# Output projection of an attention layer: from four fp32 products on token chunks to three two-part products with stationary weights

## The reference, cut to what matters

```
q, k, v = (split_heads(layernorm(x) @ W) for W in (Wq, Wk, Wv))
attn = softmax(q @ k.T + bias)
ctx = (attn @ v)                 # per head 512 x 64, 16 heads: 512 x 1024
x = x + ctx @ Wo                 # Wo: 1024 x 128
```

## Time and profile before

| | |
|---|---|
| runs timed | 1105.16 us median of 3 (1104.22 to 1105.43) |
| the profiled execution's own time | 1105.33 us |
| its span, first to last instruction | 1103.4 us |
| attention steps 0 to 63 | from 16.4 to about 780 us of the span |
| expert blocks | from there to the end |
| mean granted TensorE clock | 0.985 |

### The profile page before, as it was taken

How to read it: one execution, slowest core, us unless ns; L and a number is a source line. 1 busy time by engine, 2 the same in 40 slices (tenths; PEclk the granted TensorE clock), 3 DMA queues, 4 the chain that set the end, 5 groups by cost and what they waited for, 6 DMA issues and landing times.

```text
span 1103.4 us, 26950 instructions
## 1 busy us (share of the span) xinstructions
PE 1048.9 (95%) x8345; PEld 851.4 (77%) x8346; DVE 839.2 (76%) x2610; ACT 829.6 (75%) x2040; POOL 682.4 (62%) x900
## 2 busy tenths in 40 slices
PE   8999999999999999999999999999897889999992
PEld 4777777777777777777777777777797878999991
DVE  6888888889888888888888888887474544456684
ACT  5888888788888888788788888877674546766660
POOL 3654456765775676577577657747666665566552
PEclk9999999999999999999999999999999899999996
DMA  7576666775776676677577666778423322222554
GB/s 214 160 213 187 194 170 174 215 207 164 213 204 181 176 227 193 168 221 204 159 202 222 184 176 199 236 241 253 154 80 113 97 66 71 65 70 80 181 153 153
DMA packets 135192, 188.61 MB, mean 171 GB/s; under 512 B 18599, under 2 KB 108464, under 8 KB 135056
## 3 DMA queue, kind: packets, MB, share of 16 engines
q1 hardware_dynamic: 126352, 170.01, 54.0%
q0 software_dynamic: 8704, 16.93, 4.5%
HBM read 100.52 MB, written 87.39 MB: 170 GB/s over the span
## 4 chain that ended last, share of the span: by engine, by line
PE 84%; DVE 5%; issue 3%; another core or an unknown queue 2%; DMA 2%; ACT 1%; SPq 1%; POOL 1%; DVEq 0%; POOLq 0%; ACTq 0%
PE bank L1567 16%; PE bank L1581 10%; PE bank L1749 10%; PE bank L1620 10%; PE bank L1636 10%; PE bank L1647 5%; PE bank L1518 4%; PE bank L1520 4%; PE bank L1519 4%; PE bank L1735 2%; PE bank L1733 2%; PE bank L1734 2%; PE bank L1705 1%; DVE yb L1414 1%
## 5 line engine op out<-in xcount | busy, mean ns | idle before, releaser
L984 POOL TENSOR_SCALAR shared<-shared,rinv 128x512 f32<-128x512 f32 x512 | 351.8, 699 | 243.5 <-DVE rinv L1249 240.9
L1058 ACT ACTIVATE shared<-shared,nmax 128x512 f32<-128x512 f32 x512 | 368.5, 733 | 73.0 <-DVE nmax L1243 52.9
L1243 DVE CUSTOM_DVE_ANT_0 shared<-bank,shared 128x512 f32<-128x512 f32 x512 | 330.1, 682 | 85.9 <-issue 35.0
L1025 POOL DMA_INDIRECT y_dram<-yb,home x144 | 155.4, 1079 | 111.4 <-issue 90.2
L1749 PE MATMUL bank<-shared,act_h 128*128 x1152 | 147.3, 282 | 19.1 <-DVE yb L1414 15.1
L1265 DVE STREAM_TRANSPOSE turned<-shared 128x512 f32<-128x512 f32 x248 | 160.9, 687 | 0.0
L1064 ACT ACTIVATE pt_e<-bank 128x512 f32<-128x512 f32 x256 | 144.9, 594 | 19.0 <-PE bank L1581 18.6
L399 POOL DMA_INDIRECT xs_dram<-copies,slot x128 | 134.2, 1049 | 39.1 <-issue 28.1
L1749 PEld LDWEIGHTS bank<-shared,act_h 128*128 128x128 f32 x1152 | 138.1, 196 | 24.6 <-issue 24.3
L1581 PE MATMUL bank<-idn,shared 128*128 128x128 f32 x1024 | 136.8, 276 | 0.5 <-DVE nmax L1243 0.5
L1581 PEld LDWEIGHTS bank<-idn,shared 128*128 128x128 f32 x1024 | 112.8, 141 | 24.0 <-issue 14.5
(11 more groups left out here) (229 smaller groups left out, 1876.9 us busy)
## 6 DMA issues: line engine op xcount, KB each, us to landing
pt_dram<-turned SPq DMA_DIRECT2D x496, 128.0 KB
pt_d<-pt_dram SPq DMA_DIRECT2D x124, 512.0 KB
xb<-xs_dram SPq DMA_DIRECT2D x64, 130.0 KB
shared<-in_experts SPq DMA_DIRECT2D x16, 514.0 KB
yk_sb<-y_dram SPq DMA_DIRECT2D x32, 256.0 KB
shared<-roll_dram SPq DMA_DIRECT2D x4, 768.0 KB, 8.4
y_dram<-yb,home POOLq DMA_INDIRECT x144
xs_dram<-pad_sb SPq DMA_DIRECT2D x17, 130.0 KB
```

The lines of the kernel that those rows point to most:

```text
L984: pool.tensor_scalar(tile, tile, rinv[:, 2 * v + hh:2 * v + hh + 1], 1.0, ALU.mult, ALU.mult)\
L1025: pool.indirect_dma_start(y_dram, bass.IndirectOffsetOnAxis(ap=home[:, j, c:c + 1], axis=0), yb[:, j, c, :], None, bounds_check=last_row, ...
L1058: act.activation(prob[:, v, hh, :], prob[:, v, hh, :], ACT.Exp, bias=nmax[:, n:n + 1], scale=-1.0, accum_out=rsum[:, n:n + 1]).then_inc(ex ...
L1243: dve.tensor_tensor_reduce(prob[:, v, hh, :], score_bank(v, hh)[:], strips[:, 2 * i + hh, v * P:v * P + S], -1.0, BIG, ALU.add, ALU.min, n ...
```

## The change

The context is split into a high and a low part: ScalarE's copy writes `ctxt_hi` (fp32r), and a new VectorE instruction, `context_lo`, subtracts it from the PSUM bank and writes `ctxt_lo`. Wo is split likewise, once, in step 1. `project_out` then makes three products, with the piece of Wo stationary and all 512 tokens moving; the sum stands in `ps_o` with features on the partitions. Once per batch ScalarE copies `ps_o` to SBUF (`copy_out`), TensorE transposes it back in four pieces (`turn_out`), and VectorE's `residual` reads that. `context_lo(n-2)` is the first thing on VectorE in step n; TensorE's waits on `c_cp` become waits on its semaphore `ctxt_rdy`.

```diff
+        wo_stage = shared[:, 0:NPR * D].rearrange("p (n d) -> p n d", n=NPR)
-        wo_sb = sb("wo_sb", [P, NPR, D], stack=attn)
+        wo_hi = sb("wo_hi", [P, NPR, D], F32R, attn)
+        wo_lo = sb("wo_lo", [P, NPR, D], F32R, attn)
-        ctxt = sb("ctxt", [P, S], stack=attn)
+        ctxt_hi = sb("ctxt_hi", [P, S], F32R, attn)
+        ctxt_lo = sb("ctxt_lo", [P, S], F32R, attn)
...
-        TAIL_PE = {6: 0, 7: 1, 9: 2}
+        TAIL_PE = {7: 0, 8: 1, 10: 2}
-        TAIL_DVE = {5: (3,), 7: (4, 5, 6), 8: (7, 8, 9), 9: (10, 11, 13, 14), 10: (15, 16)}
+        TAIL_DVE = {LEAD: (0, 1, 2), 6: (3,), 8: (4, 5, 6), 9: (7, 8, 9), 10: (10, 11, 13, 14), 11: (15, 16)}
...
-        TAIL_PLAN_PE = {13: 0, 16: 1, 19: 2, 22: 3}
+        TAIL_PLAN_PE = {14: 0, 16: 1, 19: 2, 22: 3}
... (ScalarE)
             def context(b, i):
                 act.wait_ge(c_rdy, b * NPR + i + 1)
-                act.activation(ctxt[:, ::-1], ps_a[:], ACT.Copy).then_inc(c_cp, 1)
+                act.activation(ctxt_hi[:, ::-1], ps_a[:], ACT.Copy).then_inc(c_cp, 1)
+            def copy_out(b):
+                act.wait_ge(o_rdy, b + 1)
+                act.activation(xt[:], ps_o[:], ACT.Copy).then_inc(out_cp, 1)
... (step, behind weights_t of chunk 3)
+                if i == 1 and exists(b - 1):
+                    copy_out(b - 1)
                 exps(b, i, 2, 0)
...
+                if (b, i) == (0, 1):
+                    act.wait_ge(ld_wo, 16)
+                    act.activation(wo_hi[:], wo_stage, ACT.Copy).then_inc(wo_hi_rdy, 1)
... (VectorE)
+            def context_lo(b, i):
+                dve.wait_ge(c_cp, b * NPR + i + 1)
+                dve.nop(nofuse=True)
+                dve.tensor_tensor(ctxt_lo[:, ::-1], ps_a[:], ctxt_hi[:, ::-1].bitcast(F32), ALU.subtract).then_inc(ctxt_rdy, 1)
             def residual(b):
-                dve.wait_ge(o_rdy, b + 1)
+                dve.wait_ge(out_rdy, b + 1)
...
                 if (b, i) == (0, 1):
+                    dve.wait_ge(wo_hi_rdy, 1)
+                    dve.tensor_tensor(wo_lo[:], wo_stage, wo_hi[:].bitcast(F32), ALU.subtract).then_inc(wo_rdy, 1)
                     routing_constants(0)
...
             def step(b, i):
-                up = pair_after(b, i, 1)
+                two, up = before(b, i, 2), pair_after(b, i, 1)
+                if exists(two[0]):
+                    context_lo(*two)
                 scores(b, i, 0, 0)
... (TensorE)
                     if n >= 2:
-                        pe.wait_ge(c_cp, n - 1)
+                        pe.wait_ge(ctxt_rdy, n - 1)
...
             def project_out(b, i):
-                pe.wait_ge(c_cp, b * NPR + i + 1)
+                pe.wait_ge(ctxt_rdy, b * NPR + i + 1)
                 if i == 0 and exists(b - 1):
                     pe.wait_ge(res_rdy, b)
-                for c in range(TC):
-                    mm = pe.matmul(ps_o[:, c * D:(c + 1) * D], ctxt[:, c * P:(c + 1) * P], wo_sb[:, i, :],
-                                   start=(i == 0 and c == 0), stop=(i == NPR - 1), skip_group_check=True)
+                for m, (w, ctxt) in enumerate(((wo_lo, ctxt_hi), (wo_hi, ctxt_lo), (wo_hi, ctxt_hi))):
+                    mm = pe.matmul(ps_o[:], w[:, i, :], ctxt[:], start=(i == 0 and m == 0), stop=(i == NPR - 1 and m == 2))
...
+            def turn_out(b):
+                pe.wait_ge(out_cp, b + 1)
+                for c in range(TC):
+                    mm = pe.transpose(ps_o[:, c * D:(c + 1) * D], xt[:, c * P:(c + 1) * P], idn[:])
+                mm.then_inc(out_rdy, 1)
             def aside(b, i):
...
+                if i == 1 and exists(b - 1):
+                    turn_out(b - 1)
... (block_pe)
                 turn(m, j)
+                if isinstance(m, int) and m == LEAD:
+                    turn_out(LAST)
...
-    nc = bacc.Bacc("TRN2", target_bir_lowering=False, num_devices=1)
+    nc = bacc.Bacc("TRN2", target_bir_lowering=False, num_devices=1, dynamic_dma_scratch_size=8192)
```

More of the change, by code:

```diff
@@ L157, in layer_kernel @@
         params = shared[:, 0:NE * EW]
+        wo_stage = shared[:, 0:NPR * D].rearrange("p (n d) -> p n d", n=NPR)
+        assert NPR * D <= AHEAD
         attn = ctx.enter_context(ExitStack())
@@ L216, in layer_kernel @@
         c_rdy, c_cp, o_rdy, res_rdy = (sem(n) for n in ("c_rdy", "c_cp", "o_rdy", "res_rdy"))
+        out_cp, out_rdy = sem("out_cp"), sem("out_rdy")
+        ctxt_rdy, wo_hi_rdy, wo_rdy = sem("ctxt_rdy"), sem("wo_hi_rdy"), sem("wo_rdy")
         k2_rdy, kk_rdy, rk_rdy, lc_rdy = sem("k2_rdy"), sem("kk_rdy"), sem("rk_rdy"), sem("lc_rdy")
@@ L770, in run_blocks @@
             drain()
-        TAIL_PE = {6: 0, 7: 1, 9: 2}
-        TAIL_ACT = {6: 0, 8: 1}
-        TAIL_DVE = {5: (3,), 7: (4, 5, 6), 8: (7, 8, 9), 9: (10, 11, 13, 14), 10: (15, 16)}
[L775 to L778, removed]
-        TAIL_PLAN_PE = {13: 0, 16: 1, 19: 2, 22: 3}
-        TAIL_PLAN_DVE = {14: 0, 17: 1, 18: 2, 20: 3, 21: 4, 23: 5}
+        TAIL_PE = {7: 0, 8: 1, 10: 2}
+        TAIL_ACT = {7: 0, 9: 1}
+        TAIL_DVE = {LEAD: (0, 1, 2), 6: (3,), 8: (4, 5, 6), 9: (7, 8, 9), 10: (10, 11, 13, 14), 11: (15, 16)}
+        TAIL_POOL = {2: ("rstd",), 4: ("copy",)}
+        TAIL_POOL.update({9 + q: (q,) for q in range(SCATTERS)})
+        TAIL_POOL[9] = ("weights",) + TAIL_POOL[9]
+        TOTALS = 12
+        TAIL_PLAN_PE = {14: 0, 16: 1, 19: 2, 22: 3}
+        TAIL_PLAN_DVE = {15: 0, 17: 1, 18: 2, 20: 3, 21: 4, 23: 5}
         PADS = 20
@@ L822, in _ @@
             load_strips(1)
-            sp.dma_start(wo_sb[:], wo.rearrange("(n p) d -> p n d", p=P)).then_inc(ld_wo, 16)
+            sp.dma_start(wo_stage, wo.rearrange("(n p) d -> p n d", p=P)).then_inc(ld_wo, 16)
             for g in range(2, H // TC):
@@ L1185, in drain @@
                 gelu(2, 2)
+                copy_out(LAST)
             def weights_hi(n, cols):
@@ L1426, in block_dve @@
                 if isinstance(m, int):
+                    if m == LEAD:
+                        residual(LAST)
                     for stage_no in TAIL_DVE.get(m, ()):
@@ L1475, in drain @@
                 expert_lo(0, 0)
+                context_lo(LAST, NPR - 2)
                 turned_lo(1, 1)
@@ L1480, in drain @@
                 finish(0, 0)
+                context_lo(LAST, NPR - 1)
                 turned_lo(3, 3)
                 expert_lo(3, 3)
-                residual(LAST)
                 finish(1, 1)
-                for stage_no in range(3):
-                    route_dve(dve, LAST, stage_no)
             dve.wait_ge(ld_x0, 16)
@@ L1793, in step @@
                 if n == 2:
-                    pe.wait_ge(ld_wo, 16)
+                    pe.wait_ge(wo_rdy, 1)
                 if exists(two[0]):
```

## The result

The changed kernel took **1119.3 us** (median of 4 runs, 1118.2 to 1121.4) beside 1104.7 us for the kernel before on the same chip (4 runs): a ratio of 1.0137, 95% interval 1.0115 to 1.0159. The profiled execution took 1118.23 us. Forecast were 1118.3 us, slower, in 1109 to 1126. A second set of runs gave 1.0108 (1.0071 to 1.0145), so the change costs 12 to 15 us. The steps came out nearly as forecast, too; but a part of the good agreement in the sum is luck, as the experiments show.

A forecast was written before the change was run, and what follows sets the result against it. Bound: two equal paths to project_v, PE's own work and VectorE's scores. Ordinary steps 6.9, i = 5 steps 3.3, step 2 0.9, covered steps -1.1, turn_out 3.1, tail 0: +13.1 us, forecast 1118.3, range 1109 to 1126.

The forecast's parts named there:

- the saving is worth 0: project_out, steps 2 to 62: three products save 0.20 us of PE per pair, all lost waiting for VectorE's sixth score.
- `context_lo`: Start of each ordinary step on VectorE: the subtraction delays the first score and chunk-3 load, +0.13 us per step, 53 steps.
- i = 5 steps: Seven steps, batches 1 to 7, with VectorE on routing until 1.14: score 0.62 to 0.68 later, +0.47 us each.
- `turn_out`: Once per batch on PE: four transposes cost 0.44 us, 7 x 0.44 = +3.1; ScalarE's copy causes at worst 0.1 wait.
- Step 2: Splitting Wo in step 1 makes VectorE's context_lo and scores of step 2 come 1.2 late: +0.9 us, once.
- less six covered steps 1.1: Six steps where weigh_early waits for the DRAM trip hide the delay: five at 0.13, one at 0.47, so -1.1 us.
- The tail: Last pairs and expert blocks: -0.4 from the products against +0.44 from turning, new tail tables 0; one block, 3.4 us, as bound.
- A: Rival: PE's own work is the bound, so its saving comes out and the kernel gets faster, 1096.0 us; chance 0.07.
- B: Rival: context_lo fits fully into VectorE's idle 0.62; only turn_out and step 2 remain, 1105 to 1109 us; chance 0.08.
- C: Rival: VectorE becomes the bound, the subtraction's 0.68 going wholly onto the path, 1150 us; chance 0.05.
- D: Tail rival: another PE stall in the expert blocks with a half-clock stretch, +3 to +6, 1121 to 1124 us; no chance given.
- E: Rival: project_out's three products run at fp32's rate, 3 x 0.9 instead of 0.7 us, 1230 us; chance under 0.01.

The follow-up runs named there:

- half the projection: Kernel before with two of project_out's four token chunks left out; ratio 0.9993 (0.9970 to 1.0017), ordinary step 11.51 us.
- second trace: Changed kernel run once more, unchanged, to get another trace; ordinary steps 11.61 us, its first four blocks 20.6 us.

## Why the prediction was right, point by point

**What bounds the step.** "Only if both shrink does the step shrink" holds: PE 0.44 us less changes nothing (half the projection), and without the wait 0.17 comes out (order q, k, v). That the saving is worth 0 is shown by two runs: without `context_lo` the step is 11.50 with PE's saving, where the kernel before has 11.51 without it; and with `context_lo` alone it is 11.62, as in the changed kernel. What the working left out is a wait on the same path, of the chunk-3 transposes for VectorE's fifth score, 0.07 us from binding in the kernel before. It didn't touch the forecast, since the sixth score covers it; but of the "some 0.2" that PE was to wait at `project_v` it took 0.10, and 0.13 were left there. It also spoiled the forecast for half a projection in the new order.

**`context_lo`.** +0.11 where I had 0.13, by the path that I gave: first score at 1.42, chunk-3 load at 2.16, transposes 0.08 late. In i = 5 steps +0.40 where I had 0.47: `context_lo` starts at 1.14 and the score at 1.73, so the score is 0.59 late, not 0.62 to 0.68. Both terms are the subtraction's, as its removal gave them back.

**`turn_out`.** 0.43 instead of 0.44, on the path in full; the copy is free.

**Step 2.** +0.95 instead of +0.9: `wo_lo` took 1.20 us, and PE waited 0.67 for the first score. Without `context_lo` that step takes 11.85, so splitting Wo alone costs 0.34, and the rest is the subtraction behind it.

**The step that was mis-sized:** "less six covered steps 1.1". The sum came out 2.9 us below the steps' in the first trace and 2.4 in the second. I took the waits of one trace for fixed. Apart from steps 55 to 57 they come in other steps from trace to trace (15, 19, 22, 39, 47, 55 to 58 and 61 before; 15, 32, 55 to 57 and 61 in the first trace after, 21, 23, 31, 32 and 55 to 57 in the second), and their sum scatters from 3.3 to 7.4 us. It was 3.3 and 3.9 in the changed kernel and 5.7 before, but 6.3 with `context_lo` alone, whose steps are just as long. The attention part is thus +9.7, not +13.1, and I can't say how much of the difference is cover and how much chance.

**The tail.** I took 0, a term without a row behind it. The first trace had +5.5 in the blocks, of which 2.9 lay in the drain's stall and the second trace doesn't have. The second trace's blocks are 3.8 us longer than those of before all the same, and those of the variants on the slower chips lie between 7 us shorter and 6 longer. So whether the new tail tables cost something stays open; they weren't tried alone. The 13.0 us of the first trace are 9.7 in the steps, shown by the experiments but for the rest of -2.9, 5.5 in the blocks and -2.3 ahead of step 2; the last two are open but for the stall. That they add up to the 13.1 of the forecast is luck: a step part 3.4 too large, and two parts that it didn't have, together +3.2.

**The rivals.** A is out (1076 forecast for half a projection, 1105.7 measured). B is out: the loads wait for the late score 53 times. C is out for the changed kernel; only in the run with the later subtraction did VectorE lengthen some steps by more than 1.5 us, and by another cause, POOL's tiles. D came true in the first trace, with a stall of 2.07 us and a lower clock behind it, for +2.9, and not in the second; the time stayed in the range either way. E is out: the products start 0.32 and 0.23 us apart, and the three take 0.78 us, 0.08 more than I took.

## What to carry to other kernels

Before cutting an engine's work, leave half of it out and look at the step: one run showed that 29 us of the busiest engine's work were worth nothing. Where two paths of equal length meet, cut both, and look for the next wait close by, here 0.07 us from binding: list every wait of the stretch with its slack, also those that the profile shows as no wait. An operation put into another engine's idle time is free only if what comes next there could start as late as it ends.

## What had not been expected of the hardware

**Two operands in SBUF on VectorE wait for POOL.** The 128x512 subtraction took 0.67 us, and up to 2.45 while POOL worked on SBUF tiles without a pause; with an operand in PSUM it took 0.66 to 0.69 in all 64 pairs. The Trainium skill, page SBUF — State Buffer, section SBUF: two separate sides, has a rule for it: a VectorE instruction with two SBUF inputs and a GpSimd one that reads SBUF exclude each other for a whole instruction. This trace agrees with the rule in kind, but not in size: one of POOL's instructions is 0.69 us long, and VectorE's took 1.67 longer and ended only behind the third.

**Chips differ in the expert blocks.** The version with the order alone took 728 us from step 2 to step 63 in both its traces, but 297.3 us from the end of the first four blocks on one chip and 269.7 on the other, on which the kernel before took 1071 us too. Groups by line, kernel before on the first chip, then that version on the fast one:

```profile
L1749 PE MATMUL bank<-shared,act_h 128*128 x1152 | 147.3, 282 | 19.1 <-DVE yb L1414 15.1
```
```profile
L1749 PE MATMUL bank<-shared,act_h 128*128 x1152 | 140.6, 275 | 0.4 <-ACT act_h L1115 0.3
```

On the fast chip PE's idle time ahead of these products is 0.4 us instead of 19.1, and none of it is put down to VectorE's `yb`. What holds the blocks up on the other chips wasn't looked into. It is why every comparison here is within one chip.
